# Two-stage attention and routed feed-forward on one core: reordering a hand-written step and moving small operations between engines

## What is computed

```python
q = layernorm(x) @ Wq.T + bq;  k = ctx @ Wk.T + bk;  v = ctx @ Wv.T + bv   # each as 16 heads x 16
attn = softmax(q @ k.T / 4)          # 16 x 16 over the heads of ONE token
o = attn @ v                         # reshaped so that token and head are mixed
x = x + o @ Wd.T + bd
h = layernorm(x)
gates = softmax((h @ w_red) @ normalized(wg).T)      # 8 experts
e = argmax(gates);  score = max(gates)
x = x + score * (gelu(h @ W1[e] + b1[e]) @ W2[e] + b2[e])
```

## Time and profile before

| | us |
|---|---|
| median of 3 runs | 500.99 (500.74 to 502.97) |
| the profiled execution | 497.12 |
| its span, first to last instruction | 495.3 |
| its mean granted TensorE clock | 0.952 of full speed |

### The profile page before, as it was taken

One profiled execution on the slowest core, in us unless ns is written; L12 is line 12 of the kernel. 1 busy time (PEld: TensorE's weight loads), 2 busy tenths in 40 slices (PEclk: granted clock), 3 DMA queues, 4 the chain that ended last, 5 costly groups with the idle time before them and its releaser, 6 DMA issues.

```text
span 495.3 us, 9892 instructions
## 1 busy us (share of the span) xinstructions
PE 421.0 (85%) x3025; PEld 304.9 (62%) x3029; DVE 372.4 (75%) x632; ACT 265.8 (54%) x882; POOL 383.4 (77%) x369
## 2 busy tenths in 40 slices
PE   8866889798888787879888778988899999999991
PEld 6534455454454454544545445677789999999980
DVE  5999999998988989988999997236774555455440
ACT  4545678777776777878887531554221223223320
POOL 7999999997996989998999911455586677777741
PEclk9989999998997999998999967899998999999997
DMA  4626988898898898897987743732233233333310
GB/s 135 150 66 90 163 142 143 154 176 144 157 188 167 121 168 151 167 187 109 172 159 115 114 64 52 175 97 74 78 97 97 72 102 115 105 92 108 97 35 1
DMA packets 231722, 59.39 MB, mean 120 GB/s; under 512 B 204297, under 2 KB 221874, under 8 KB 231542
## 3 DMA queue, kind: packets, MB, share of 16 engines
q1 hardware_dynamic: 218502, 36.37, 43.9%
q0 software_dynamic: 4992, 14.51, 10.1%
q10 hardware_dynamic: 8176, 7.87, 5.4%
HBM read 37.68 MB, written 21.96 MB: 120 GB/s over the span
## 4 chain that ended last, share of the span: by engine, by line
PE 41%; DVE 30%; DMA 9%; issue 6%; ACT 5%; SPq 4%; POOL 2%; DVEq 1%; ACTq 0%; POOLq 0%
DVE bL L214 12%; PE bQ L1006 12%; PE bL L981 6%; PE bKV L981 6%; PE bKV L857 4%; SPq L274 4%; DVE prod L206 4%; DMA a_scr<-a 3%; DMA row_scr<-cat 3%; PE bQ L888 3%; DMA aexp<-a_scr 2%; PE bO L871 2%; DVE a L463 2%; PE bT L990 1%; DVE sm L457 1%
## 5 line engine op out<-in xcount | busy, mean ns | idle before, releaser
L206 POOL TENSOR_TENSOR prod<-q,kk 128x2048 f32<-128x2048 f32 x64 | 235.5, 3703 | 13.3 <-issue 12.8
L214 DVE TENSOR_REDUCE bL<-prod 128x128 f32<-128x2048 f32 x64 | 143.3, 2284 | 0.0
L1006 PE MATMUL bQ<-w,prod 128*128 x312 | 74.6, 382 | 2.8 <-DVE prod L685 2.6
L857 PE MATMUL bKV<-wT,xcT 128*128 128x512 f32 x128 | 66.9, 649 | 5.0 <-ACT xcT L739 5.0
L1006 PEld LDWEIGHTS bQ<-w,prod 128*128 128x128 f32 x312 | 56.2, 190 | 11.0 <-issue 4.8
L406 POOL DMA_INDIRECT out<-prod,isc x39 | 41.4, 1062 | 20.2 <-issue 20.2
L801 ACT ACTIVATE prod<-bKV,prod 128x128 f32<-128x128 f32 x80 | 22.9, 368 | 57.4 <-PE bKV L981 57.4
L685 DVE TENSOR_TENSOR prod<-bQ,b2b 128x256 f32<-128x256 f32 x39 | 16.5, 424 | 48.2 <-PE bQ L1006 45.3
L801 ACT ACTIVATE prod<-bL,prod 128x128 f32<-128x128 f32 x76 | 21.7, 368 | 47.4 <-PE bL L981 47.4
L399 POOL DMA_INDIRECT prod<-row_scr,ig x39 | 41.7, 1070 | 5.8 <-issue 2.2
L910 PE MATMUL bY<-wT,oT 128*128 128x256 f32 x128 | 39.0, 430 | 6.4 <-ACT oT L780 6.3
(11 more groups left out here) (212 smaller groups left out, 766.0 us busy)
## 6 DMA issues: line engine op xcount, KB each, us to landing
row_scr<-cat SPq DMA_DIRECT2D x32, 258.0 KB, 4.4
v_scr<-vs SPq DMA_DIRECT2D x32, 128.0 KB, 4.3
w1b<-in_L_ffn_W SPq DMA_DIRECT2D x8, 512.0 KB, 4.5
w<-in_L_ffn_W SPq DMA_DIRECT2D x8, 512.0 KB, 4.3
a_scr<-a SPq DMA_DIRECT2D x32, 128.0 KB
v<-v_scr SPq DMA_DIRECT2D x32, 128.0 KB, 3.9
aexp<-a_scr SPq DMA_DIRECT2D x128, 32.0 KB, 2.8
xt<-in_x ACTq DMA_DIRECT2D x15, 256.0 KB, 3.6
```

Of the source, the lines that this page charges most:

```text
L206: return eng.tensor_tensor(prod[t % 2][:, lo:hi, :].rearrange("p i (j d) -> p i j d", j=NH), q_[:, lo * HD:hi * HD].rearrange("p (i d) -> ...
L214: return eng.tensor_reduce(lg[t % 2][:, h * HALF:(h + 1) * HALF, :], prod[t % 2][:, h * HALF:(h + 1) * HALF, :] .rearrange("p i (j d) -> p ...
L857: eng.matmul(bKV[:, :], xcT[:, KC + k, :], wT[:, k, C:3 * C], start=(k == 0), stop=False)
L1006: i_ = eng.matmul(bQ[:, 0:C], hT[b % 2][:, k, :], w2[:, bass.ds(eb * (KH * C) + k * C, C)], start=(k == 0), stop=(k == KH - 1))
```

## The change

Six edits:

- **Order on TensorE.** K and V of tile t move to the head of step t, ahead of the `xn` transposes. The context transposes of tile t+1 are made in step t, after the product with V. Q and the gate logits come right after the transposes, ahead of the product with V. Wd stays at the end of the step.
- **Order on ScalarE.** `xcT` is copied in two parts: the `x` part (now semaphore `xT`) in its old place, the context part (`cT`) of the next tile after `oT`. `kk` and `vs` come ahead of the moments of tile w, `q` comes ahead of `oT`.
- **Work moved from VectorE.** The residual is added on TensorE by a product of the identity with `xt` into `bY`, and ScalarE copies `bY` to the row. The maximum logit is taken with its sign changed, at the head of VectorE's step, and ScalarE subtracts it. The sum of the gate exponentials is written to the row itself, and the reciprocal is taken later, once for each slot of the feed-forward part.
- **Heads.** GpSimd multiplies 12 heads, VectorE four.
- **DMA queue.** The loads of `x` and context go from ScalarE's queue to SyncE's, at the head of a step.
- **Layout of `v_scr`.** V is written as whole rows, and the read picks it apart, where before the write did.

```diff
@@ -21,7 +21,7 @@
-POOLH = 13
+POOLH = 12
...
-    v_scr = nc.dram_tensor("v_scr", [NT, NH, P, HD], f32, kind="Internal").ap()
+    v_scr = nc.dram_tensor("v_scr", [NT, P, C], f32, kind="Internal").ap()
...
         def sync_attention(eng):
             for t in range(LAST + 1):
                 v, e, u, g = t - 1, t - 3, t - 4, t - 9
+                n = t + 2
+                if live(n) and n % 2 == 0:
+                    if n >= XR:
+                        eng.wait_ge(S["x2"], n - XR + 2)
+                    eng.dma_start(xt[:, n % XR:n % XR + 2, :], x[n:n + 2].rearrange("n p c -> p n c")
+                                  ).then_inc(S[f"ld_x{n // 2 % 2}"], 16)
+                    if n >= 4:
+                        eng.wait_ge(S["tr_c"], n - 2)
+                    eng.dma_start(ct[:, n % 4:n % 4 + 2, :], ctx_in[n:n + 2].rearrange("n p c -> p n c")
+                                  ).then_inc(S[f"ld_c{n // 2 % 2}"], 16)
                 if live(v):
                     eng.wait_ge(S["vcp"], v + 1)
-                    eng.dma_start(v_scr[v].rearrange("j t d -> t j d"), vs[v % 2][:, :]
-                                  .rearrange("p (j d) -> p j d", d=HD)).then_inc(S[f"st_v{v % 2}"], 16)
...
                     eng.dma_start(v2[u % 2][:, :].rearrange("p (l z) -> p l z", z=2 * HD)[:, :, 0:HD],
-                                  v_scr[u].rearrange("j (b l) d -> (j b) l d", b=NB)
+                                  v_scr[u].rearrange("(b l) (j d) -> j b l d", b=NB, d=HD)
                                   ).then_inc(S[f"ld_v{u % 2}"], 16)
...
         def vector_attention(eng):
             for t in range(LAST + 1):
-                v, b, e, w, g = t - 1, t - 2, t - 3, t - 6, t - 8
+                v, b, e, g = t - 1, t - 2, t - 3, t - 8
                 if t == NT + 3:
                     vector_early(eng, 3)
+                if live(g):
+                    eng.wait_ge(S["glg"], g + 1)
+                    if g > 0:
+                        eng.wait_ge(S["gsub"], g)
+                    eng.tensor_reduce(gm[:, :], bG[:, C:C + NE], AX, ALU.max, negate=True).then_inc(S["gm"], 1)
...
-                if live(g):
-                    eng.wait_ge(S["glg"], g + 1)
-                    eng.tensor_reduce(gm[:, :], bG[:, C:C + NE], AX, ALU.max).then_inc(S["gm"], 1)
-                    eng.wait_ge(S["gm"], g + 1)
-                    eng.tensor_scalar(glog[:, g, :], bG[:, C:C + NE], gm[:, :], None,
-                                      ALU.subtract).then_inc(S["gsub"], 1)
...
-                if live(w):
-                    eng.wait_ge(S["wd"], w + 1)
-                    if w >= CR:
-                        eng.wait_ge(S[f"st_r{w % CR}"], w // CR * 16)
-                    eng.tensor_tensor(cat[w % CR][:, C:2 * C], bY[:, 0:C], xt[:, w % XR, :],
-                                      ALU.add).then_inc(S["x2"], 1)
...
-                if 0 <= g < R1:
-                    eng.wait_ge(S["gexp"], g + 1)
-                    eng.reciprocal(cat[g % CR][:, 2 * C:2 * C + 1], gs[:, :]).then_inc(S["score"], 1)
...
-                eng.tensor_reduce(gs8, ge8, AX, ALU.add).then_inc(S["rv_s"], 1)
-                eng.wait_ge(S["rv_s"], 1)
-                eng.reciprocal(sc8[:, :], gs8).then_inc(S["score8"], 1)
+                eng.tensor_reduce(sc8[:, :], ge8, AX, ALU.add).then_inc(S["score8"], 1)
...
+                eng.reciprocal(rsc[b % 2], gr[b % RB][:, 2 * C:2 * C + 1]).then_inc(S["rsc"], 1)
...
-                eng.scalar_tensor_tensor(yo[k], yb[b % 2], gr[b % RB][:, 2 * C:2 * C + 1], gr[b % RB][:, C:2 * C],
+                eng.wait_ge(S["rsc"], b + 1)
+                eng.scalar_tensor_tensor(yo[k], yb[b % 2], rsc[b % 2], gr[b % RB][:, C:2 * C],
...
+                if live(g):
+                    eng.wait_ge(S["gm"], g + 1)
+                    eng.activation(glog[:, g, :], bG[:, C:C + NE], ACT.Identity, bias=gm[:, :]).then_inc(S["gsub"], 1)
...
                 if live(a):
+                    if a == 0:
+                        scalar_context(eng, 0)
                     eng.wait_ge(S["tr_in"], a + 1)
                     if a > 0:
-                        eng.wait_ge(S["kv"], a)
                         eng.wait_ge(S["qq"], a)
-                    eng.activation(xcT[:, :, :], bT[:, :].rearrange("p (a c) -> p a c", a=4),
-                                   ACT.Copy).then_inc(S["xcT"], 1)
+                    eng.activation(xcT[:, 0:KC, :], bT[:, 0:C].rearrange("p (a c) -> p a c", a=KC),
+                                   ACT.Copy).then_inc(S["xT"], 1)
                 if live(d):
...
+                if live(w):
+                    eng.wait_ge(S["wd"], w + 1)
+                    if w >= CR:
+                        eng.wait_ge(S[f"st_r{w % CR}"], w // CR * 16)
+                    eng.activation(cat[w % CR][:, C:2 * C], bY[:, 0:C], ACT.Copy).then_inc(S["x2"], 1)
                 if live(a + 1):
                     front(eng, a + 1)
-                if live(w):
-                    eng.wait_ge(S["x2"], w + 1)
-                    moments(eng, w, 1, cat[w % CR][:, C:2 * C])
...
-                if 0 <= g < R1:
-                    eng.wait_ge(S["gsub"], g + 1)
-                    if g > 0:
-                        eng.wait_ge(S["score"], g)
-                    eng.activation(ge[:, :], glog[:, g, :], ACT.Exp, accum_out=gs[:, :]).then_inc(S["gexp"], 1)
-                n = t + 2
-                if live(n) and n % 2 == 0:
-                    if n >= XR:
-                        eng.wait_ge(S["x2"], n - XR + 2)
-                    eng.dma_start(xt[:, n % XR:n % XR + 2, :], x[n:n + 2].rearrange("n p c -> p n c")
-                                  ).then_inc(S[f"ld_x{n // 2 % 2}"], 16)
-                    if n >= 4:
-                        eng.wait_ge(S["tr_c"], n - 2)
-                    eng.dma_start(ct[:, n % 4:n % 4 + 2, :], ctx_in[n:n + 2].rearrange("n p c -> p n c")
-                                  ).then_inc(S[f"ld_c{n // 2 % 2}"], 16)
...
                     eng.activation(vs[a % 2][:, :], bKV[:, C:2 * C], ACT.Copy).then_inc(S["vcp"], 1)
+                if live(w):
+                    eng.wait_ge(S["x2"], w + 1)
+                    moments(eng, w, 1, cat[w % CR][:, C:2 * C])
+                if 0 <= g < R1:
+                    eng.wait_ge(S["cat0"], CR)
+                    eng.wait_ge(S["gsub"], g + 1)
+                    eng.activation(ge[:, :], glog[:, g, :], ACT.Exp,
+                                   accum_out=cat[g % CR][:, 2 * C:2 * C + 1]).then_inc(S["score"], 1)
+                if live(a):
+                    eng.wait_ge(S["qq"], a + 1)
+                    eng.activation(q[a % 2][:, :], bQ[:, 0:POOLH * HD], ACT.Copy).then_inc(S["qcp"], 1)
                 if live(c):
...
-                if live(a):
-                    eng.wait_ge(S["qq"], a + 1)
-                    eng.activation(q[a % 2][:, :], bQ[:, 0:POOLH * HD], ACT.Copy).then_inc(S["qcp"], 1)
+                if live(a + 1):
+                    scalar_context(eng, a + 1)
                 if live(b):
                     eng.wait_ge(S["lsub"], b + 1)
                     eng.activation(pr[b % 2], lg[b % 2], ACT.Exp, scale=HD ** -0.5).then_inc(S["exp"], 1)
...
+
+        def scalar_context(eng, a):
+            eng.wait_ge(S["tr_c"], a + 1)
+            if a > 0:
+                eng.wait_ge(S["kv"], a)
+            eng.activation(xcT[:, KC:2 * KC, :], bT[:, C:2 * C].rearrange("p (a c) -> p a c", a=KC),
+                           ACT.Copy).then_inc(S["cT"], 1)
...
+        def tensor_context(eng, a):
...
...
         def tensor_attention(eng):
             for t in range(LAST + 1):
                 a, c, d = t, t - 5, t - 7
                 if live(a):
-                    eng.wait_ge(S[f"ld_c{a // 2 % 2}"], (a // 4 + 1) * 16)
                     if a > 0:
-                        eng.wait_ge(S["xcT"], a)
+                        eng.wait_ge(S["vcp"], a)
+                    else:
+                        tensor_context(eng, 0)
+                        fill(eng, 4)
+                        eng.wait_ge(S["wT"], 2)
+                    eng.wait_ge(S["cT"], a + 1)
                     for k in range(KC):
-                        i_ = eng.transpose(bT[:, (KC + k) * P:(KC + k + 1) * P], ct[:, a % 4, k * P:(k + 1) * P],
-                                           ident[:, :])
-                    i_.then_inc(S["tr_c"], 1)
+                        eng.matmul(bKV[:, :], xcT[:, KC + k, :], wT[:, k, C:3 * C], start=(k == 0), stop=False)
+                    if a == 0:
+                        eng.wait_ge(S["ld_br"], 16)
+                        eng.wait_ge(S["ones"], 1)
+                    eng.matmul(bKV[:, :], ones[0:3, :], brow[:, C:3 * C], start=False, stop=True).then_inc(S["kv"], 1)
+                if live(a):
                     eng.wait_ge(S["xn"], a + 1)
...
                 if live(a):
                     if a > 0:
-                        eng.wait_ge(S["vcp"], a)
+                        eng.wait_ge(S["qcp"], a)
```

(45 more changed lines are left out.)

24 lines of the change are left out of this document (15 added, 9 removed).

## The result

| | before | after |
|---|---|---|
| median of four runs, us | 501.98 (500.74 to 503.63) | 514.63 (513.44 to 516.21) |
| ratio | | 1.0265, 95% interval 1.0215 to 1.0314 |
| profiled execution, us | 497.12 | 513.44 |
| its span, us | 495.3 | 511.6 |

The change makes the kernel 2.65% slower. The forecast was 517.4 us on the median and 513.5 on the profiled execution.

What follows compares the result with a forecast made beforehand. A ScalarE-TensorE loop of 9.02 us would bound attention: 26 intervals +12.1, first three -0.7, clock +5, sum +16.4 us, giving 513.5 us profiled and 517.4 on the median. Range 491 to 550 us, the forecast's own 510 to 530.

Steps and rivals of the forecast that it cites:

- The ring: Loop through ScalarE and TensorE in attention, from one tile's `xT` copy to the next tile's: 9.02 us a step.
- its bounds: Loop length 8.9 us with each copy 0.26 and a free start, 9.4 with two 0.2 us semaphore hiccups.
- the stretch: Full attention steps from GpSimd's score product 5 to product 31: 26 intervals, 222.45 us before the change.
- the old loop: Loop through ScalarE and TensorE before the change, `xcT` of one tile to the next: terms summing to 8.33 us.
- less 0.7: First three of the 26 attention intervals lack parts of the loop: -0.7 us.
- "+5" for the clock: Attention work at 1.2 GHz, about 13 us by the earlier granted clock, slows the new loop: +5 us.
- the new gap before Wd: TensorE stands still from the context transposes' end until Wd starts after `oT`: near 1.7 us in each step.
- the rival of 0.13: TensorE's gaps bring the low clock often: 557 us if half the steps pay, 535 if a quarter; chance 0.13.
- the sign for being right: In attention, GpSimd's products 9.0 us apart with over 1.5 us idle between; VectorE idle over 1 us a step.
- 1.6 us of cover: Time in each attention step by which `aexp` may delay the product with V before `oT` is late: costed at nothing.
- Start and drain: Steps 0 to 4, without `oT`, and the end of attention: each 0, the drain between -2 and +2 us.
- the engines stay the bound: VectorE's 7.81 us sets the attention step because the loop closes sooner: -12.4 us, 488.6 us, faster; chance 0.18.

Runs made afterwards that it cites:

- the fill: Ten dummy transposes, which nothing reads, put ahead of Wd's bias product on TensorE in the changed kernel: 504.91 us, ratio 1.0070 against the kernel before.
- the 13th head: The changed kernel with GpSimd multiplying 13 heads again and VectorE three: 517.64 us, ratio 1.0291 against the kernel before.

## Why the prediction was right

**The ring.** The prediction's sum was 9.02, its bounds 8.9 and 9.4; it measured 8.92. Term by term, from the rows of one round above: ScalarE from `xT` to `oT` 4.49 (4.54 predicted), `oT` to Wd 0.43 (0.44), Wd and identity 1.40 (1.46), K and V with bias 2.12 (2.16), transposes to copy 0.48 (0.42). The run with K and V behind the transposes takes the 2.12 out, down to VectorE's step, and gains 25.9 us; the one without identity and copy takes 0.70 a step out and gains 23.4 by the medians, of which 26 x 0.70 = 18 are this (in the profiles the stretch is 19.0 us shorter and the start 2.0). So the mechanism was tested from two sides. The prediction's reason for taking 9.02, that the same sum gives the old loop exactly, was no test: distances between the time stamps of one round add up to that round whatever sets it.

**The sum was right partly by luck.** For the stretch I had 238.8 us (234.5, less 0.7, plus 5) and 240.0 came. The ring was 0.1 shorter (-2.6), the first two intervals were shorter by more than I took off (-1.6), the last one lacks a tile's moments (-1.5), and the clock cost 11.6, not 5 (+6.6). That is the mis-sized term: "+5" for the clock, taken over from the share of 1.2 GHz before. The six late intervals have (10.57 + 10.61 + 10.62 + 10.57 + 10.58 + 10.61) - 6 x 8.92 = 10.0 us, and the last one 1.55. The four errors cancel to 1 us. That 513.5 was met by 513.44 is luck in part for a second reason: by the medians the change costs 12.65 us (514.63 less 501.98), not 16.4, and the forecast of 517.4 is 2.8 too high. I had named the new gap before Wd in each step (1.7 us; it is 1.42), but only as the rival of 0.13, with a quarter or half of the steps at +3.5 each. It is 7 of 26, the quarter, but at +1.67 each, half of my price: the low clock lasts through Wd, identity and part of K and V and is over at the transposes. That rival's mechanism was thus present, with 11.6 us where I gave it 23 for a quarter of the steps and 45 for half, and the fill shows that it is the gap that brings it.

**The engines.** VectorE idles 1.17 us and GpSimd 1.43 a step (1.2 and 1.6 predicted; the sign for being right asked for over 1.5 on GpSimd). VectorE's own step, seen where it is the bound, is 7.66 (7.81 predicted). The fourth head cost 1222 less 950 ns, 0.27 (0.28).

**Waits and queues.** `aexp` was costed at nothing with 1.6 us of cover. In after that holds: one wait of 1.1 us. The kernels with a shorter ring and steps under 8.8 us waited 3 to 15 us for it from 60 to 270 us. The layout of `v_scr` and the 13th head leave the full step as it is, as said; by the medians they are 2 and 3 us over after. **Start and drain** were put at 0 and gave -0.4 and -0.9.

**The rival "the engines stay the bound"** had 488.6 us for its result; the kernel with K and V behind the `xn` transposes is that kernel, at 488.7. The mechanism is the rival's, the equal number is luck: its stretch is 218.45 us and not 210, and by the profiled executions it gains 5.9 us where the rival's sum has 12.4. The change holds a gain and hides it by one order of calls. The Trainium skill's rule (Perfetto Trace Analysis, Identifying the Most-Contended Engine), to start with the engine of the highest occupancy, is not enough in this trace: what was taken off VectorE and GpSimd bought nothing as long as the ring stood. With the ring out of the way the kernel was 2.9% faster than before.

## What to carry to other kernels

Before an instruction is moved in a program written by hand, follow every ring that runs through two engines' orders (from one tile's copy to the next tile's) and sum it: the longest of these sums and of the engines' own steps decides (before, 8.33 and 8.28 us lay side by side), and an idle engine whose program lies in a ring is not free. When one bound is lifted, look up how much cover the DMA round trips had under it; here the next wait was for a store and eight loads through one queue, 1.6 us away. A gap on TensorE in every step can cost time beyond its length, through the clock; compare the same instructions in several steps for it.
